# Turning all attention probabilities by VectorE blocks and transfers instead of half of them on TensorE

## The reference

```python
x = x + tanh(g_xattn) * xattn(layernorm(x), ctx, ...)          # first layer, not touched
x = x + tanh(g_ffn) * ffn(layernorm(x), Wq, Wk, Ws, Wd, Wv, Wo)
# ffn, with 8 heads of 64, 5 experts, 2 picked:
q, k   = x @ Wq, x @ Wk                                        # by head
wv     = topk_mask(x @ Ws, 2) * sigmoid(x @ Ws)
v      = einsum('bthe,btek->bhtk', wv, einsum('btd,edk->btek', x, Wv))
probs  = softmax(q * scale @ k.T)                              # 512 x 512 for each head
attn   = probs @ v
out    = einsum('bthe,bthk,ekd->btd', topk_mask(x @ Wd, 2), attn, Wo)
```

## Time and profile before

| | |
|---|---|
| median of 3 runs | 1153.29 us (1152.88 to 1154.09) |
| the profiled execution | 1152.18 us, of which its span is 1150.4 us and 1.78 us lie around it |
| TensorE busy in the span | 1120.2 us, 97% |
| VectorE | 904.9 us, 79% |
| ScalarE | 588.6 us, 51% |
| GpSimd | 658.0 us, 57% |
| transfers, share of 16 engines | 31% |
| granted TensorE clock | 1.00 |

### The profile page before, as it was taken

The page is one execution under the profiler, slowest core; times in us unless marked ns, Lnnn a source line. Parts: engine busy times, 40 slices in busy tenths (PEclk is TensorE's granted clock), DMA queues, the critical chain, the costliest instruction groups (busy, mean ns, idle before and its releaser), DMA issues.

```text
span 1150.4 us, 19136 instructions
## 1 busy us (share of the span) xinstructions
PE 1120.2 (97%) x5885; PEld 856.2 (74%) x5885; DVE 904.9 (79%) x1656; ACT 588.6 (51%) x1332; POOL 658.0 (57%) x476
## 2 busy tenths in 40 slices
PE   7999999999999999999999999999999999999998
PEld 6888888888888888886666767767667666767655
DVE  7998787878787866578597797786887876976977
ACT  7634443434444344447455555555556545565543
POOL 2645252525252524329759579389398498496694
DMA  5441414141414132343324323324225233242241
GB/s 202 147 138 46 138 46 128 55 128 55 128 55 128 55 91 92 129 129 74 91 56 129 88 51 117 91 55 130 71 58 161 55 91 111 55 122 59 55 128 38
DMA packets 76606, 108.44 MB, mean 94 GB/s; under 512 B 7712, under 2 KB 40224, under 8 KB 76576
## 3 DMA queue, kind: packets, MB, share of 16 engines
q1 hardware_dynamic: 76576, 108.07, 31.0%
HBM read 58.76 MB, written 16.78 MB: 66 GB/s over the span
## 4 chain that ended last, share of the span: by engine, by line
PE 68%; POOL 13%; DVE 8%; issue 6%; ACT 4%; DVEq 0%; DMA 0%; POOLq 0%; ACTq 0%; SPq 0%
PE ps_f L992 23%; PE ps_s L992 8%; PE ps_o L2274 7%; PE ps_h L992 7%; POOL spare L1587 6%; PE ps_r L2200 6%; POOL spare L1593 5%; PE ps_r L2233 5%; PE ps_s L2251 4%; PE ps_r L2209 3%; DVE nmax L1860 3%; PE ps_s L2259 2%; DVE z_tmp L1879 2%; ACT probs_odd L1670 1%; POOL z L1605 1%
## 5 line engine op out<-in xcount | busy, mean ns | idle before, releaser
L1860 DVE TENSOR_REDUCE nmax<-ps_s 128x1 f32<-128x512 f32 x256 | 158.5, 680 | 79.0 <-PE ps_s L2251 78.0
L1587 POOL TENSOR_TENSOR spare<-xv,pick 128x512 f32<-128x512 f32 x160 | 184.8, 1155 | 35.0 <-DVE pick L1975 22.1
L1605 POOL TENSOR_TENSOR z<-z,z_tmp 128x1280 f32<-128x1280 f32 x35 | 102.6, 2932 | 138.6 <-DVE z_tmp L1879 136.3
L1593 POOL TENSOR_TENSOR spare<-spare 128x512 f32<-128x512 f32 x128 | 165.6, 1294 | 10.0
L1670 ACT ACTIVATE tmp<-ps_s,nmax 128x512 f32<-128x512 f32 x124 | 85.2, 687 | 97.1 <-DVE nmax L1860 97.1
L2274 PE MATMUL ps_o<-pt,spare 128*64 128x512 f32 x496 | 113.3, 598 | 6.6 <-POOL spare L1593 5.1
L254 POOL TENSOR_TENSOR e_t<-e_t 128x512 fp32r<-128x512 f32 x28 | 35.4, 1300 | 135.7 <-ACT e_t L510 135.7
L2251 PE MATMUL ps_s<-k,q 64*128 64x512 f32 x768 | 106.4, 408 | 3.1 <-ACT pt L1679 3.1
L2251 PEld LDWEIGHTS ps_s<-k,q 64*128 64x128 f32 x768 | 67.3, 184 | 49.3 <-issue 33.3
L254 POOL TENSOR_TENSOR c<-stage,c 128x512 fp32r<-128x512 f32 x28 | 42.3, 1542 | 94.4 <-ACT c L250 94.4
L2200 PE MATMUL ps_r<-es_t,c_t 128*128 128x512 f32 x384 | 96.3, 399 | 0.0
(11 more groups left out here) (245 smaller groups left out, 2272.2 us busy)
## 6 DMA issues: line engine op xcount, KB each, us to landing
pt<-tmp SPq DMA_DIRECT2D x248, 128.0 KB, 2.6
stage<-in_x SPq DMA_DIRECT2D x32, 256.0 KB, 3.2
x_sb<-in_x SPq DMA_DIRECT2D x8, 1024.0 KB, 5.3
x_dram<-x_sb SPq DMA_DIRECT2D x32, 256.0 KB, 3.1
stage<-x_dram SPq DMA_DIRECT2D x8, 1024.0 KB, 5.4
x_sb<-x_dram SPq DMA_DIRECT2D x8, 1024.0 KB, 5.4
out_dram<-x_sb SPq DMA_DIRECT2D x31, 256.0 KB, 2.6
stage<-in_ctx_t SPq DMA_DIRECT2D x28, 256.0 KB, 2.8
```

The costliest lines, as they stand in the source:

```text
L1587: pool.tensor_tensor(v_tmp[:] if e else acc, xv[:, :, e, :].unsqueeze(2).broadcast_to(shape), pick[:, e, :, 2 * p:2 * p + 2].unsqueeze(3). ...
L1593: pool.tensor_tensor(acc, acc, v_tmp[:], ALU.add).then_inc(v_steps, 1)
L1605: pool.tensor_tensor(zv, zv, z_tmp[:, h % 2], ALU.add).then_inc(z_pool, 1)
L1860: dve.tensor_reduce(nmax[:, n:n + 1], ps_s[:, n % BANKS, :], AX_X, ALU.max, negate=True).then_inc(nmax_ready, 1)
```

## The change

- Odd tiles no longer go through TensorE and ScalarE. All four tiles of a round are written in blocks into one buffer of 2048 columns (two such buffers, one of them new). VectorE turns them in two transposes of 1024 columns each where it had two of 512, and the four transfers of a round carry 256 KB each where they had 128 KB. The bank of a tile is free when its exponential is taken.
- `turn_blocks` moves from the place TURNS to AFTER, the last of VectorE's round.
- `coefficients` moves from VectorE to GpSimd: pair 0 behind `mix_values` 1, pair 1 and pair 2 behind `mix_sums` 0 and 1, pair 3 ahead of `mix_sums` 2; and `mix_sums` 0 moves ahead of `mix_values` 3. For the last two pairs of the last batch they stay on VectorE.
- The copy of the norm moves from VectorE to ScalarE, ahead of its first normed tile.
- turn_z moves from BEHIND to AFTER of round 11, and TensorE takes the newer batch's AFTER first there, so that turn_z comes behind values 0 of the next batch.
- The last two rounds of the last batch still turn all four tiles on TensorE.

```diff
-        AT["turn_z", k] = (11, BEHIND)
+        AT["turn_z", k] = (11, AFTER)
...
+        def blocks(n):
+            return probs[n // BANKS % 2].rearrange("p (j i s a) -> p j i s a", i=2, s=2, a=BLOCK)[:, :, n % 2,
+                                                                                              n % BANKS // 2, :]
...
                 for q in range(QUADS):
+                    sp.dma_start(by_rows(p)[:, r % 2, q].rearrange("p k i s a -> p (k i s a)"),
+                                 probs[r % 2][q * BLOCK:(q + 1) * BLOCK].rearrange(
+                                     "p (j u) -> p j u", j=QUADS)).then_inc(moved[r % 2], 16)
...
+            def coefficients(b, p):
+                heads = slice(2 * p, 2 * p + 2)
+                pool.wait_ge(rden_ready, b * PAIRS + p + 1)
+                if p == 0:
+                    pool.wait_ge(mask_ready, b + 1)
+                pool.tensor_tensor(coef[:, heads], ..., ALU.mult).then_inc(coef_ready, 1)
...
             def rest(b, first=False):
-                for p in range(1, PAIRS):
-                    mix_values(b, p, first)
-                for p in range(LAST_PAIR - 1):
-                    mix_sums(b, p)
+                mix_values(b, 1, first)
+                coefficients(b, 0)
+                mix_values(b, 2, first)
+                mix_sums(b, 0)
+                coefficients(b, 1)
+                mix_values(b, 3, first)
+                mix_sums(b, 1)
+                coefficients(b, 2)
...
             with pool.Fori(0, B - 2) as b:
+                coefficients(b, LAST_PAIR)
                 mix_sums(b, LAST_PAIR - 1)
...
             def normalise(b, tiles):
+                if tiles[0] == 0:
+                    act.wait_ge(last_newton, ROOT_STEPS + 1)
+                    act.activation(norm[:], x1_norm[:, :, bass.ds(b * NT, NT)], ACT.Copy).then_inc(norm_ready, 1)
...
+                if n % BANKS == 0 and (n >= 2 * BANKS or not first):
+                    act.wait_ge(moved[n // BANKS % 2], (b * PAIRS + n // PAIR) * MOVED)
+                act.activation(blocks(n), ps_s[:, n % BANKS, :].rearrange("p (j a) -> p j a", a=BLOCK), ACT.Exp,
+                               bias=nmax[:, n:n + 1], accum_out=den[:, h, t:t + 1]).then_inc(p_exp, 1)
-
-            def probs_copy(b, n, first):
...
+            def turn_blocks(b, r, i):
+                dve.wait_ge(p_exp, b * STEPS + r * BANKS + i + 3)
+                both_tiles = probs[r % 2].rearrange("p (j i u) -> p j i u", i=2, u=2 * BLOCK)[:, :, i, :]
+                dve.transpose(both_tiles, both_tiles).then_inc(blocks_turned, 2)
...
                 elif place == TURNS:
-                    if 0 <= n < ROUNDS:
-                        for tile in range(n * BANKS, n * BANKS + BANKS, 2):
-                            turn_blocks(b, tile)
...
                 elif place == BEHIND:
                     units_lo(b, units_at(n, BEHIND, AFTER, table=FIRST_AT if first else AT), first)
+                elif 0 <= n < ROUNDS:
+                    for i in range(2):
+                        turn_blocks(b, n, i)
...
-                    pe.wait_ge(pt_ready, odd_turned(b, n + 1 - BANKS))
+                    pe.wait_ge(p_exp, b * STEPS + n + 2 - BANKS)
...
-                    elif place == TURNS:
-                        for tile in range(n * BANKS + 1, n * BANKS + BANKS, 2):
-                            turn_probs(b, tile)
...
                 for n in range(CUT, CUT + ROUNDS):
-                    for place in PLACES:
+                    for place in PLACES[:AFTER]:
                         step(b, n, place)
                         step(b + 1, n - ROUNDS, place)
+                    step(b + 1, n - ROUNDS, AFTER)
+                    step(b, n, AFTER)
```

More of the change, by code:

```diff
@@ L87 @@
     spare: object
+    late: object
     tmp: object
@@ L1627, in _ @@
                 rest(b + 1)
+            coefficients(B - 2, LAST_PAIR)
             mix_sums(B - 2, LAST_PAIR - 1)
@@ L1630, in _ @@
                 mix_values(B - 1, p)
+                if p in (1, 2):
+                    coefficients(B - 1, p - 1)
             everything, second_tiles = slice(0, NT), HALVES[1][1]
             last_sum(3, everything, 0, 2)
-            pool.wait_ge(coef_ready, B * PAIRS)
+            pool.wait_ge(last_coef, 2)
             last_sum(4, everything, 1, 2)
@@ L1658, in scores_exp @@
                 h, t = head_tile(n)
-                scores = ps_s[:, n % BANKS, :]
-                if n % 2 == 0:
-                    if n >= 2 * BANKS or not first:
-                        act.wait_ge(moved[n // BANKS % 2], (b * PAIRS + n // PAIR) * MOVED)
-                    out, scores = even_probs(n), scores.rearrange("p (j a) -> p j a", a=BLOCK)
-                else:
-                    if n >= BANKS or not first:
-                        act.wait_ge(pt_ps, odd_turned(b, n - BANKS))
-                    out, scores = plainly(probs_odd[:, n % BANKS // 2, :]), scores_by_keys(scores)
-                act.activation(out, scores, ACT.Exp, bias=nmax[:, n:n + 1],
-                               accum_out=den[:, h, t:t + 1]).then_inc(p_exp, 1)
-            def probs_copy(b, n, first):
-                h, t = head_tile(n)
-                act.wait_ge(pt_ps, odd_turned(b, n))
-                if t == 0 and (h >= 4 or not first):
-                    act.wait_ge(o_ps, b * PAIRS + h // 2 - 1)
-                act.activation(turned(n), scored(n), ACT.Copy).then_inc(pt_ready, 1)
+                if n % BANKS == 0 and (n >= 2 * BANKS or not first):
+                    act.wait_ge(moved[n // BANKS % 2], (b * PAIRS + n // PAIR) * MOVED)
+                act.activation(blocks(n), ps_s[:, n % BANKS, :].rearrange("p (j a) -> p j a", a=BLOCK), ACT.Exp,
+                               bias=nmax[:, n:n + 1], accum_out=den[:, h, t:t + 1]).then_inc(p_exp, 1)
             def last_exp(b, n):
@@ L1985, in step @@
                 if place == SCORES:
-                    if n == NORMALISE_AT and not first:
-                        take_norm(b)
                     for p in range(PAIRS):
@@ L2080, in last_rounds @@
                     row_max(b, n)
-                coefficients(b, 2)
+                last_coefficients(b, 2)
                 for h in (2, 3):
@@ L2088, in last_rounds @@
                 row_sums(b, 3)
-                coefficients(b, 3)
+                last_coefficients(b, 3)
                 last_mix(5, turned_pair(2))
@@ L2299, in values_half @@
                     for a in range(2):
-                        rows = by_rows(p % 2 * 2 + a)[:, half, :, k].rearrange("p q s a -> p q (s a)")
+                        rows = by_rows(p)[:, half, :, k, a].rearrange("p q s a -> p q (s a)")
                         end = pe.matmul(out[head_rows(a)], v_acc[:, p, k, a, :], rows, start=k == 0, stop=k == NT - 1)
```

75 lines of the change are left out of this document (26 added, 49 removed).

## The result

The changed kernel takes 1193.09 us (median of 4 runs, 1192.22 to 1203.36) where the kernel before took 1153.09 beside it (4 runs): ratio 1.0367, 95% interval 1.0310 to 1.0424, slower by 3.7%. The ratio is that of the means and the one run of 1203.36 lifts it; the medians lie 3.5% apart. The profiled execution takes 1193.49 us, with a span of 1191.7.

A forecast was written before the change was run, and what follows sets the result against it. By busy time TensorE bounds the kernel; VectorE's and GpSimd's order would then decide. Six passes at +4.7 us (28.2), +5.3 for the first batch and +4 at the end, on 1152.2, gave 1189.7, said as 1190; range 1160 to 1217.

The forecast's parts named there:

- the case that I held likeliest: Whole kernel: the round-by-round timing holds and VectorE's and GpSimd's order slows it to 1178 to 1202 us; chance 0.56.
- a sign that I had named for being wrong: TensorE at values 0: a wait for GpSimd under 2 us would refute the forecast, which had 6 to 7 us.
- The turn's price: VectorE, each round: two wide transposes take 2.29 us instead of 1.22, with bounds of 1.22 and 2.44.
- Coefficients on GpSimd: GpSimd's list: 0.4 us each, bounds nothing and 1.1; with mix_sums 0 ahead, mix_values 3 ends at 62.4 us.
- Rounds 10 and 11: Counted from round 9's maximum (D9), round 11's (D11) comes at 20.1 us and round 12's (D12) at 34.15.
- Rounds 12 to 8: Maxima from round 9's: round 12 at 34.15 us, 8 at 75.5; round 8's turn adds its full 2.29.
- the walk: One pass timed round by round from one maximum of round 9 to the next: 85.9 us against 81.2.
- The pass: One loop pass takes 85.9 us against 81.2, +4.7; six of these intervals add 28.2.
- The first batch: Ahead of the first round 9 maximum: later pick, mix_sums 0 and two coefficients, less transposes saved: +5.3 us.
- The end: Behind the last round 9 maximum: +2.9 us in round 5 and +1.1 for a wide turn before transfers, +4.
- The clock: TensorE's idle in round 11 halves its clock at values 0: +3.6 us a pass, 1215 us; chance 0.13.
- TensorE stays the bound: Whole kernel: TensorE's saved transposes shorten a pass by 3.4 us, giving 1128 us; chance 0.11.

The follow-up runs named there:

- the run with three groups of idle transposes: Changed kernel with unused TensorE transposes ahead of round 10's scores, turn_y 0 and values 0, so no long wait there is idle: 1188.29 us, ratio 1.0299.
- The reordered queue: Changed kernel with SyncE's transfers of round 5 of the last batch issued ahead of the last residual's load: 1189.35 us, ratio 1.0321.
- small moves alone: Kernel before with only coefficients on GpSimd, mix_sums 0 ahead of mix_values 3 and the norm on ScalarE: 1187.58 us, ratio 1.0299.
- both with z behind: Changed kernel, turn_z still behind values 0, with the wide transposes back in the place TURNS: 1169.93 us, ratio 1.0155.
- the mixed kernel: Kernel before with only rounds 12, 5, 6 and 7 turned wide, in TURNS: 1158.40 us; with the norm on ScalarE too, 1144.31 us.

## Why the prediction was right, and where it was not

1190 was said, 1193.1 measured, in the case that I held likeliest. The mechanism stands in the main: VectorE's list between rounds 8 and 12, together with GpSimd's chain to values 0, replaces TensorE as the bound, and TensorE's relief shows in waits and in round 7, 11.2 us for 12.1. But a sign that I had named for being wrong came true, a wait of TensorE at values 0 under 2 us (1.28, on average 1.6), and 1190 came nearer than its parts: the passes are 2.2 us below what I said, the first batch 1.3 below and the end 7.3 above.

- **The turn's price**, 2.29 a round: measured 1.22 a transpose and 2.28 between the starts of the pair's first and what follows it. Right. The Trainium skill ("VectorE: DVE Perf Modes", Rules for kernel authors) would have kept the transposes on TensorE. All eight rounds wide do lose, alone as well, but with four of eight, and the norm on ScalarE, the kernel wins, so here it depends on the round, according to which engine has slack.
- **Coefficients on GpSimd**: 0.27 each for my 0.4. Right in kind. The terms that I gave for the end of mix_values 3 add up to 62.2, not 62.4; measured were 61.6.
- **Rounds 10 and 11.** I had the largest step in round 11, 13.9 for 11.3 (34.15 less 20.1 is 14.05). It is in round 10, 11.94 for 9.15; round 11 takes 11.44. D11 came 1.6 later than I said, for two reasons. I wrote "TensorE has made the scores before" of round 10: wrong. Those scores belong to the next head pair and wait for VectorE's low part of k, which stands behind its products. So 3.73 of the wait lies there, the clock falls there, q comes late, and VectorE idles 0.85 for it. The rest is VectorE's sum of z beside GpSimd, 2.45 for 1.63. The error ends at D11: VectorE waits for z in round 11 anyway, only 1.81 instead of my 4.8, and with D11 1.3 earlier, in the run with three groups of idle transposes, D12 is still at 33.2. D12 hangs on GpSimd's chain, which was 1.2 sooner than before (values 0 at 23.72 for 24.95), and so it came 1.0 earlier than I said. GpSimd's products beside VectorE's sums of z took 2.18 instead of 1.05 twice before and once now, because the second sum starts behind the chain's end. GpSimd's timeline in the kernel before, then VectorE's and GpSimd's in the changed one:

```profile
758.84 2.17 POOL L1587 TENSOR_TENSOR spare<-xv,pick 128x512 f32<-128x512 f32 x1
...
764.97 2.18 POOL L1587 TENSOR_TENSOR spare<-xv,pick 128x512 f32<-128x512 f32 x1
```

```profile
772.85 2.45 DVE L1874 TENSOR_TENSOR z<-z,z_tmp 128x1280 f32<-128x1280 f32 x1
774.02 2.18 POOL L1579 TENSOR_TENSOR spare_late<-xv,pick 128x512 f32<-128x512 f32 x1
```

- **Rounds 12 to 8**: each round within 0.6 of the walk and each maximum within 0.9; the turn in front of the next D9 is there as said, and the run with turns in TURNS shows that its place makes the cost.
- **The pass**, +4.7 said, +4.3 measured. The first batch, +5.3 said, +4.0 measured.
- **The end**, +4 said, +11.3 measured. This term was mis-sized most: I had counted the wide turn ahead of the transfers, but not what stands ahead of them in SyncE's queue. The reordered queue took back 3.7 us of it in time and 4.4 of the wait. The rest, as far as the traces go, is transfers of 256 KB that take longer from issue to use (8.3 us, 7.1 with the load behind them, for 4.65), values 2 at a low clock (6.61 for 3.65), and the turn's place: with the turns in TURNS, 86.7 us follow the last D9 instead of 93.3.
- **The clock** did fall, as that rival had it, but not where and not at its price. The run without rests puts it at 0.9 us a pass for my 3.6. TensorE was busy for 76.4 us of a pass for my 71; without the fall it has 72.1 (82.0 in the run with three groups, less their 9.9). With a wait of 4.85 in front of values 0, in the run with half of a turn left out, they took 2.9 longer, which is nearer to my price. The Trainium skill ("TensorE: Matmul & The Clock Gate", The HAM clock gate) says that idleness lowers the clock; this trace agrees, 0.94 granted in the pass for 1.00.
- **TensorE stays the bound**, the rival of the other sign, failed on the point named for it: from D8 to D12 the way grew from 37.8 to 43.4 us.

What stays open: the parts don't add. Wide turns alone cost 32 us, small moves alone 35, both with z behind 17, and the turn's place 23 more. The traces name the waits for each, but I ran no kernel with the wide turns and only the norm or only the coefficients moved, so how the 14 us between the wide turns alone and the run with turns in TURNS split among z, norm, coefficients and the order of mix_sums isn't shown. Nor was the mixed kernel tried with other rounds, such as 12 and 7 alone.

## What to carry to other kernels

Before moving work from a full engine to one at 80%, write down round by round how long the receiver waits ahead of its next shared result; move only into these waits, and put the moved work ahead of the wait, not behind it. Follow the order of every list that feeds the bound, the transfer queue's too. When taking work off changes nothing, look for a second chain of the same length before giving the theory up.

## What the runs showed of the hardware

- A small VectorE instruction between SBUF tiles can end with the GpSimd instruction beside it: 1.28 us for 8 columns, ending at 784.24, where GpSimd's sum ended at 784.21. In the trace of before the same copy took 0.38, but it too ended at 785.90 with a sum of GpSimd that ended at 785.88 (timeline of both engines):

```profile
784.59 1.29 POOL L1593 TENSOR_TENSOR spare<-spare 128x512 f32<-128x512 f32 x1
...
785.52 0.38 DVE L1856 TENSOR_SCALAR norm<-x_norm 128x8 f32 x1
```

- VectorE's sum of z and GpSimd's products take longer where they overlap: 2.45 us for 1.63 and 2.18 for 1.05, in the lines above.
- TensorE's clock fell within a pass. Rests of 2.7, 3.9, 4.9 and 11.4 us were followed by 5.18, 4.99, 6.51 and 6.61 for the 16 matmuls of values that take 3.65 at the full clock. Behind the rest of 1.3 in front of values 0 they took 3.65. A longer rest isn't always followed by slower matmuls: behind 9.21 they took 4.97, behind 6.68 they took 6.57.
- A transpose in blocks of 1024 columns takes 1.22 us, of 512 columns 0.68, so width costs 1.05 ns a column.
